# Transposed scores eight groups behind the maxima instead of ten, in an attention and feed-forward kernel on one core

## What is computed

```
h = x @ W1 + b1;  q, k, v = h by heads (16 heads, 8 wide)
w = softmax(where causal: q . k / sqrt(8));  y = x + (w . v) @ Wp + bp
h = (y - mean(y)) / sqrt(var(y) + eps)
prev = h shifted by one token
xr = mu_r * h + (1 - mu_r) * prev;  xk = mu_k * h + (1 - mu_k) * prev
z = h + sigmoid(xr @ Wr.T) * (relu(xk @ Wk.T) ** 2 @ Wv.T)
out = (z - mean(z)) / sqrt(var(z) + eps)
```

## Time and profile before

| | |
|---|---|
| runs, median (lowest to highest) | 651.06 us (650.29 to 652.81) |
| profiled execution | 650.12 us |
| its span, first to last instruction | 648.4 us |
| granted TensorE clock, mean | 0.976 |
| busy: TensorE, VectorE, ScalarE, GpSimd | 564.7, 550.0, 451.1, 413.6 us |
| weight loads of TensorE | 243.9 us |
| chain that ended last, by engine | TensorE 38%, VectorE 28%, GpSimd 14%, ScalarE 7%, issue 6%, DMA 5% |

### The profile page before, as it was taken

How to read it: one execution, slowest core, us unless ns; L and a number is a source line. 1 busy time by engine, 2 the same in 40 slices (tenths; PEclk the granted TensorE clock), 3 DMA queues, 4 the chain that set the end, 5 groups by cost and what they waited for, 6 DMA issues and landing times.

```text
span 648.4 us, 17196 instructions
## 1 busy us (share of the span) xinstructions
PE 564.7 (87%) x6438; PEld 243.9 (38%) x6438; DVE 550.0 (85%) x1579; ACT 451.1 (70%) x878; POOL 413.6 (64%) x576
## 2 busy tenths in 40 slices
PE   3457888999999999999999999999999999997864
PEld 1122333444343534343443444343434344342333
DVE  1477789999999999999999999999999999894437
ACT  2102777777787878787878778787878787776831
POOL 4100425667778686767767786867777777757673
PEclk9999999999999999999999999999999999997965
DMA  4652262525355443726264545436362535410101
GB/s 169 116 148 51 84 135 77 140 52 149 85 148 101 134 101 116 134 85 135 51 168 81 149 103 147 95 125 116 117 126 64 133 66 148 85 37 3 33 17 33
DMA packets 70825, 65.78 MB, mean 101 GB/s; under 512 B 14357, under 2 KB 60502, under 8 KB 70742
## 3 DMA queue, kind: packets, MB, share of 16 engines
q1 hardware_dynamic: 70178, 64.22, 41.2%
q10 hardware_dynamic: 564, 0.46, 0.3%
HBM read 34.70 MB, written 29.88 MB: 100 GB/s over the span
## 4 chain that ended last, share of the span: by engine, by line
PE 38%; DVE 28%; POOL 14%; ACT 7%; issue 6%; DMA 5%; SPq 2%; DVEq 0%; POOLq 0%; ACTq 0%
DVE rowmax L813 16%; PE ops L606 12%; PE sps L579 8%; POOL probs L1021 6%; PE tps L541 5%; PE spare L502 4%; POOL scaled L1059 4%; PE sps L564 4%; ACT probs L730 3%; POOL mixed L1063 3%; PE spare L482 3%; PE spare L516 2%; DMA d_parts<-qk_parts 2%; DVE stats L819 2%; DVE attnT L876 2%
## 5 line engine op out<-in xcount | busy, mean ns | idle before, releaser
L813 DVE TENSOR_REDUCE rowmax<-sps 128x1 f32<-128x512 f32 (+7 forms) x1024 | 395.6, 444 | 36.0 <-PE sps L579 34.7
L730 ACT ACTIVATE probs<-tps 128x512 f32<-128x512 f32 x640 | 347.6, 598 | 98.0 <-PE tps L541 95.4
L1021 POOL TENSOR_SCALAR_AFFINE_SELECT probs<-probs 128x512 f32<-128x512 f32 x256 | 158.6, 637 | 172.8 <-ACT probs L730 172.2
L606 PE MATMUL ops<-probs,vop 128*32 128x384 f32 (+3 forms) x2048 | 173.7, 446 | 15.9 <-ACT osum L736 8.1
L579 PE MATMUL sps<-kop,qop 48*64 48x512 bf16 (+7 forms) x2048 | 130.0, 309 | 12.1 <-DMA kop<-d_parts 12.1
L541 PE MATMUL tps<-qop,kop 50*128 50x384 bf16 (+3 forms) x1024 | 126.7, 306 | 12.3 <-ACT probs L730 11.6
L564 PE MATMUL sps<-qmask,dup 64*128 64x128 bf16 (+1 forms) x640 | 69.8, 215 | 28.2 <-DVE rowmax L813 25.9
L541 PEld LDWEIGHTS tps<-qop,kop 50*128 50x128 bf16 x1024 | 34.2, 94 | 147.7 <-ACT probs L730 122.8
L606 PEld LDWEIGHTS ops<-probs,vop 128*32 128x32 f32 x2048 | 50.4, 109 | 79.5 <-issue 41.5
L579 PEld LDWEIGHTS sps<-kop,qop 48*64 48x64 bf16 x2048 | 43.0, 106 | 53.4 <-issue 21.7
L564 PEld LDWEIGHTS sps<-qmask,dup 64*128 64x128 bf16 x640 | 31.3, 94 | 75.2 <-DVE rowmax L813 70.7
(11 more groups left out here) (111 smaller groups left out, 501.0 us busy)
## 6 DMA issues: line engine op xcount, KB each, us to landing
qop<-d_parts SPq DMA_DIRECT2D x64, 192.0 KB, 4.5
kop<-d_parts SPq DMA_DIRECT2D x63, 192.0 KB, 5.0
d_parts<-qk_parts SPq DMA_DIRECT2D x15, 768.0 KB, 3.4
d_parts<-qk_parts SPq DMA_DIRECT2D x15, 512.0 KB, 4.6
d_parts<-qk_parts SPq DMA_DIRECT2D x17, 256.0 KB, 4.6
xT<-x_by_channel SPq DMA_DIRECT2D x16, 256.0 KB, 2.6
xres<-x SPq DMA_DIRECT2D x16, 256.0 KB, 3.5
out<-result SPq DMA_DIRECT2D x15, 256.0 KB, 2.5
```

The costliest lines, as they stand in the source:

```text
L606: last = nc.tensor.matmul(ops[32 * t:32 * t + 32, BLK * a:SEQ], vop[:, par, a, QUARTET * half + t, hh, :], probs[:, g % 2, i, off:off + w] ...
L730: nc.scalar.activation(probs[:, g % 2, i, :], tps[:, bank(n), :], ACT.Exp, scale=SCALE)\
L813: last = nc.vector.reduce_max(rowmax[:, par, QUARTET * half + i, a:a + 1], sps[:, bank(n), off:off + w], axis=AX_X)
L1021: last = nc.gpsimd.affine_select(out=v, in_=v, compare_op=ALU.is_ge, fill=0.0, base=0, pattern=[[0, QUARTET], [1, BLK]], channel_multiplie ...
```

## The change

It sets `LEAD` to 2, so the stages T, D, E and F run two groups earlier against S. A is split: making q and k stays with A, now one step sooner (offset 3, groups 8 and 9, first step -3), while storing, splitting and loading their parts is a stage L with the old offset. Against the transposed scores, q and k, their splits, project, key, gate and hT keep their groups; v0 goes from late group 6 to 5, v1 from 9 to 6, value from 5 to 9. On VectorE and GpSimd, transposing and splitting the maxima go ahead of their group's work; z, its moments and its inverse deviation come four, two and one groups later (z behind value); both halves of `h` are made in late group 6. On GpSimd the second scaling of the mixing goes from late group 9 to 0 and its sum to 1, the bias sum to 3, the square to 5. On ScalarE `copy_o` goes ahead of the group's spare use. On SP the load of the residual input goes behind the maxima of half 0, and the loads of half 0's operands no longer wait until half of the maxima are made. The core of the diff:

```diff
-OFFSET = {"X": 3, "A": 2, "S": 1, "T": 0, "D": -1, "E": -2, "F": -3}
-FIRST_STEP, LAST_STEP = -2, 17
+OFFSET = {"X": 3, "A": 3, "L": 2, "S": 1, "T": 0, "D": -1, "E": -2, "F": -3}
+FIRST_STEP, LAST_STEP = -3, 17
...
-    ("A", "q"): (0, 0), ("A", "k"): (1, 0),
-    ("S", "v0"): (6, 0), ("S", "v1"): (9, 0),
+    ("A", "q"): (8, 0), ("A", "k"): (9, 0),
+    ("S", "v0"): (3, 0), ("S", "v1"): (4, 0),
     ("D", "project"): (4, 0), ("D", "hT"): (7, 0),
-    ("E", "key"): (2, 0), ("E", "gate"): (3, 0), ("E", "value"): (5, 0),
+    ("E", "key"): (2, 0), ("E", "gate"): (3, 0), ("E", "value"): (9, 0),
...
-LEAD = 0
+LEAD = 2
...
# SP
-                    if active("S", b):
-                        wait(sp, s_done, 4 * GROUPS * before("S", b) + 2 * GROUPS)
...
                 if active("S", b):
                     load_max(other, 0, 2 * before("S", b))
+                if active("D", b + 1):
+                    wait(sp, xbias_done, before("D", b + 1))
+                    sp.dma_start(xres[:], ...).then_inc(xres_in, 16)
...
# ScalarE
-                        for _, use, n in ORDER[b, g, place]:
-                            spare_use(use, n)
                         if place == 0 and tg == 1 and active("D", tb):
                             copy_o(before("D", tb), 1)
                         if place == 0 and tg == CHUNKS + 1 and active("T", tb):
                             copy_o(before("T", tb), 0)
+                        for _, use, n in ORDER[b, g, place]:
+                            spare_use(use, n)
...
-                    if g in (2, 3) and active("A", b) and before("A", b) > 0:
-                        split_middle(before("A", b), g - 2)
+                    if g in (0, 1) and active("L", b):
+                        split_middle(before("L", b), g)
...
# VectorE
+                    if g == CHUNKS and active("S", b):
+                        turn_maxima(before("S", b), 0)
+                    if g == 0 and active("S", b - 1):
+                        turn_maxima(before("S", b - 1), 1)
                     if active("S", b):
                         reduce_chunk(before("S", b), g, 0)
                         reduce_chunk(before("S", b), g, 1)
-                    if g == CHUNKS and active("S", b):
-                        turn_maxima(before("S", b), 0)
-                    if g == 0 and active("S", b - 1):
-                        turn_maxima(before("S", b - 1), 1)
...
-                    if tg == 4 and active("D", tb) and before("D", tb) < LAST:
+                    if tg == 5 and active("D", tb) and before("D", tb) < LAST:
...
                         layer_norm_moments(y, 0, n, stats_done, moments_done)
-                    if tg == 9 and active("E", tb) and before("E", tb) < LAST - 1:
-                        n = before("E", tb)
+                    if tg == 6 and active("D", tb) and before("D", tb) < LAST:
+                        n = before("D", tb)
+                        wait(dve, z_done, n - 1)
+                        for half in range(2):
+                            normalise(0, n, half, y, h[:, n % 2], rstd_done, h_done)
+                    if tg == 1 and active("F", tb) and before("F", tb) < LAST - 1:
+                        n = before("F", tb)
                         wait(dve, z_done, n + 1)
                         layer_norm_moments(z, 1, n, stats2_done, moments2_done)
```

More of the change, by code:

```diff
@@ L408, in step @@
                 par, other = b % 2, 1 - b % 2
-                if active("D", b):
-                    wait(sp, xbias_done, before("D", b))
-                    sp.dma_start(xres[:], x[b + OFFSET["D"]].rearrange("(t p) e -> p t e", p=P)).then_inc(xres_in, 16)
                 if active("S", b):
@@ L421, in step @@
                     load_max(par, 1, 2 * before("T", b) + 1)
-                if active("X", b):
+                if active("X", b) and before("X", b) > 0:
                     n = before("X", b)
@@ L425, in step @@
                     sp.dma_start(xT[:, n % BANKS], xT_in[b + OFFSET["X"]]).then_inc(xT_loaded[n % BANKS], 16)
-                if active("A", b) and before("A", b) == 0:
+                if active("L", b) and before("L", b) == 0:
                     for i in range(2):
@@ L437, in step @@
                     load_operand(sp, par, 0, 1, 0)
-                elif active("A", b):
-                    n = before("A", b)
+                elif active("L", b):
+                    n = before("L", b)
                     wait(sp, qk_split, 2 * (n + 1))
@@ L456, in step @@
                     load_max(other, 0, 2 * before("S", b))
+                if active("D", b + 1):
+                    wait(sp, xbias_done, before("D", b + 1))
+                    sp.dma_start(xres[:], x[b + 1 + OFFSET["D"]].rearrange("(t p) e -> p t e", p=P)).then_inc(xres_in, 16)
                 if active("F", b) and before("F", b) < LAST:
@@ L612, in step @@
             def step(b):
-                if b == 1 - OFFSET["A"]:
+                if b == -OFFSET["L"]:
                     setup_rest()
@@ L751, in step @@
             def step(b):
[L752 to L755, removed]
                 for g in range(GROUPS):
                     tb, tg = late(b, g)
+                    if (b, g) == (-OFFSET["L"], 2):
+                        act.wait_ge(first_out[1], 48)
+                        load_operand(act, 0, 0, 1, 1)
+                        setup_rest()
                     for place in range(2):
@@ L888, in step @@
                     tb, tg = late(b, g)
-                    if active("S", b):
-                        reduce_chunk(before("S", b), g, 0)
-                        reduce_chunk(before("S", b), g, 1)
                     if g == CHUNKS and active("S", b):
@@ L895, in step @@
                         turn_maxima(before("S", b - 1), 1)
+                    if active("S", b):
+                        reduce_chunk(before("S", b), g, 0)
+                        reduce_chunk(before("S", b), g, 1)
                     for _, use, n in ORDER[b, g, 0]:
@@ L906, in step @@
                         divide(before("T", tb), 0)
-                    if tg == 6 and active("D", tb) and before("D", tb) < LAST:
-                        normalise(0, before("D", tb), 1, y, h[:, before("D", tb) % 2], rstd_done, h_done)
                     if active("S", b):
@@ L1067, in step @@
                     tb, tg = late(b, g)
+                    if g == CHUNKS and active("S", b):
+                        split_max(before("S", b), 0)
+                    if g == 0 and active("S", b - 1):
+                        split_max(before("S", b - 1), 1)
+                    if g == 2 and active("L", b):
+                        split_low(before("L", b), 1)
+                    if tg == 0 and active("F", tb) and before("F", tb) < LAST - 1:
+                        n = before("F", tb)
+                        is_read(pool, "value", n)
+                        wait(pool, result_done, n)
+                        nc.gpsimd.tensor_tensor(z[:].rearrange("p t e -> p (t e)"), gated[:],
+                                                h[:, n % 2].rearrange("p t e -> p (t e)"), ALU.add).then_inc(z_done, 1)
                     if tg == 0 and active("E", tb) and before("E", tb) < LAST:
+                        mix_scale(before("E", tb), 0)
+                    if tg == 1 and active("E", tb) and before("E", tb) < LAST:
                         mix_add(before("E", tb), 0)
[L1070 to L1075, removed]
+                    if tg == 3 and active("D", tb):
                         n = before("D", tb)
@@ L1083, in step @@
                                                 ALU.add).then_inc(xbias_done, 1)
-                    if tg == 3 and active("E", tb) and before("E", tb) < LAST:
+                    if tg == 5 and active("E", tb) and before("E", tb) < LAST:
                         n = before("E", tb)
@@ L1087, in step @@
                         nc.gpsimd.tensor_tensor(ksq[:], krelu[:], krelu[:], ALU.mult).then_inc(ksq_done, 1)
-                    if tg == 5 and active("D", tb) and before("D", tb) < LAST:
+                    if tg == 6 and active("D", tb) and before("D", tb) < LAST:
                         inverse_deviation(0, before("D", tb), moments_done, vareps_done, rstd_done)
[L1090 to L1095, removed]
                     if tg == 8 and active("D", tb) and before("D", tb) < LAST:
@@ L1100, in step @@
                         mix_add(before("D", tb), 1)
-                        mix_scale(before("D", tb), 0)
                     if active("T", tb):
                         mask_group(before("T", tb), tg)
-                    if g == 3 and active("A", b):
-                        split_low(before("A", b), 0)
-                    if g == CHUNKS and active("S", b):
-                        split_max(before("S", b), 0)
-                    if g == 0 and active("S", b - 1):
-                        split_max(before("S", b - 1), 1)
+                    if tg == 2 and active("F", tb) and before("F", tb) < LAST - 1:
```

(4 more changed lines are left out.)

6 lines of the change are left out of this document (removed).

## The result

The changed kernel takes 662.29 us (661.02 to 664.9, four runs) where the kernel before, on the same chip, takes 650.67 (the three runs and a fourth, 649.69): a ratio of 1.0179, 95% interval 1.0139 to 1.022. It is slower by 11.6 us; 3.9 us faster was forecast. The profiled execution took 662.04 us with a span of 660.3, so the spans differ by 11.9.

The account below looks back on a forecast made before the run. The prediction took TensorE and VectorE to bound the kernel in turns, neither full. Its terms, -8.4-0.5-0.7+8.6-0.8-1.0-1.1 = -3.9, took 651.06 to 647.2, said as 647 us, range 638 to 654.

Parts of the forecast that it names:

- VectorE has 25.2 us of work: Steady batch, rest of k to the maximum freeing late group 9: 25.2 us against 25.5 before, so no difference there.
- GpSimd's other moves lie in its idle time: GpSimd, busy 26.0 of 35.3 us: its moves cost nothing; without that cover late masks hold output matmuls up to 1.3.
- The fill: Before the first transposed score: q and k hidden, v0's 0.24 gained, transposed scores sooner; -8.4, bounds -5.5 to -9.
- Late group 9: Last group of a batch's transposed scores: first mask to next batch 3.32, before 2.60; +0.72 a batch, +8.6 over 12.
- The waits: TensorE's waits for mask (0.19) and output copy (0.53) vanish but gain nothing; about 0.5 for a maximum in late groups 2, 3.
- Batch 0: First batch of transposed scores: late group 1 meets a short pair, -0.5.
- Batches 1 and 14: Batch 1 has no value, gated or z yet, -0.7; batch 14 has no q and k, -0.8 (-2.5 to +0.7).
- Batch 15: Last batch: its first two groups now run beside maxima groups 8 and 9; -1.0 (-3 to +1).
- rival 1: Steady batches: VectorE alone sets the step, a batch stays at 35.3; 638.6 us, chance 0.22.
- The rule weighed: Judging TensorE by weight loads makes VectorE the limit and the 0.72 vanish: -12.5 in place of -3.9; not followed.
- Rival 2: Late group 0: half 0's maxima come back late, TensorE waits about 1 us in 14 batches; 660 us, chance 0.12.
- Rival 3: Fill: q and k not hidden, start not sooner, the fill gives 5.5; 650 us, chance 0.13.

Follow-up runs that it names:

- both edits: Changed kernel with GpSimd's bias sum back in late group 2 and its late group 6 mask waiting for both halves of h: 643.33 us, ratio 0.9874.
- experiment three: The run of both edits, made to the changed kernel: 643.33 us, ratio 0.9874 to the kernel before.
- experiment nine: From experiment six, value moved from late group 9 to late group 8: 653.14 us, ratio 1.0018.
- experiment two: Changed kernel with only GpSimd's mask of late group 6 made to wait for both halves of h: 653.94 us, ratio 1.0043.
- experiment six: From experiment three, the moments of z put ahead of the rest of k on VectorE in late group 1: 634.83 us, ratio 0.976.
- experiment seven: From experiment three, value moved to late group 5, v0 and v1 to late groups 8 and 9: 675.18 us, ratio 1.0387.
- a third: The edit of experiment six on top of both edits, run again with more rounds: 634.92 us, ratio 0.9737.

## Why the prediction was wrong

**The step that failed** is "VectorE has 25.2 us of work", with "GpSimd's other moves lie in its idle time" at nothing. The 25.2 was summed from durations that the division and `h` have while GpSimd leaves them alone. Whether they keep them depends on what GpSimd does at that moment, and the change moved both engines' work. They measured 0.79 and 0.64 a batch more, 1.43 in all: from the rest of k to that maximum VectorE is busy 26.8 us in the changed kernel (348.31 to 375.87) and 25.4 with both edits (341.88 to 368.01 of experiment three), and idle 0.7 in both, where 1.1 was counted. For GpSimd's moves I asked who waits for their results (late masks, up to 1.3) and not whom they hold up while they run.

The Trainium skill (SBUF — State Buffer, Who interferes with whom) states this: VectorE and GpSimd share a pair of ports, a VectorE instruction with two SBUF inputs contends with a GpSimd one that reads SBUF and not with one that only writes, a tensor_scalar from and to SBUF can contend too (in its faster two-port modes), a tensor_reduce never, and the second to issue waits for the first. The traces agree for the division beside the bias sum (1.20), beside the square (0.82) and beside the write (0.42), and for `h` beside the mask (0.66); the reductions, which here read PSUM and not SBUF, keep their durations within 0.06 beside any of them. They differ in one point, and there the measurement decides: GpSimd's scaling also reads SBUF and doesn't block the division, as these rows of the kernel before show (GpSimd, then VectorE); in all fourteen batches where it lies within a scaling it takes 0.41.

```profile
405.95 1.57 POOL L1059 TENSOR_SCALAR scaled<-step_d,scalars 128x512 f32<-128x512 f32 x1
```
```profile
407.00 0.41 DVE L869 TENSOR_TENSOR attn<-turned,inv 128x256 f32<-128x256 f32 x1
```

**The fill was right**: -8.4 forecast, -8.93 measured. The first score matmul of the maxima starts at 21.70 (21.82 before), so the rest of k costs nothing and the bound of -9 is nearly reached.

**Late group 9 was right in itself.** From its first mask matmul to the next batch it takes 379.24-375.92 = 3.32, as summed from the earlier trace rows:

```profile
375.92 0.23 PE L562 MATMUL sps<-qmask,dup 64*128 64x128 bf16 x2 [0.17 <-DVE rowmax L809]
376.08 0.41 PE L577 MATMUL sps<-kop,qop 48*64 48x384 bf16 x8
376.42 1.16 PE L480 MATMUL spare<-value_weights,ksq 128*128 128x128 f32 x8
...
379.24 0.39 PE L539 MATMUL tps<-qop,kop 50*128 50x512 bf16 x2
```

Taking value out there wins only 0.40 of its 1.09, though, as experiment nine shows; in late group 8 all of it counts. Without the collisions the batch is 35.82 where 36.0 was forecast, +0.50 in place of +0.72, since late group 9's mask then starts 32.5 us after the batch's start, 0.2 sooner than before, where no difference was forecast. Experiment three's 643.33 is 8.2 under its kernel before, where 3.9 was forecast: the steps of the working stood but for the missing term, the sizes only roughly.

**The waits** went as foretold: those of the earlier trace rows nearly vanish, the waits for the maxima grow instead, and late groups 2 and 3 wait 0.27 and 0.28 for a maximum (about 0.5 forecast).

**The other terms.** Batch 0: -0.5 forecast, -1.0 measured. Batches 1 and 14: -0.7 and -0.8 forecast, +0.75 and +0.29 measured; late group 7 in each is as long as in the middle (3.94 and 3.99), so `h`'s 0.64 is in both. At the end of batch 1 the granted clock falls besides (0.83 in 116.00 to 119.04), and late group 9 takes 3.96 where experiment two, with the clock at 1.00, has 3.50. Without either, in experiment two, batches 1 and 14 take 34.52 and 33.95, 0.36 under the kernel before: half of what was forecast. Batch 15: -1.0 forecast, -0.22; its cause was not followed. The end: -1.1 forecast, -1.23.

**The rivals.** VectorE alone as the limit (rival 1) falls, and so does TensorE alone: experiment six won 0.77 from VectorE's order with TensorE's work as it was; experiment seven lost 0.64 in late group 8 by v0, which is no work of VectorE, and experiment nine 1.09 there by value, where VectorE then idles 0.46 for TensorE (`gated` moved along with value). They take turns, group by group. The rule weighed, of the Trainium skill (Perfetto Trace Analysis, Identifying the Most-Contended Engine), would have made the 0.72 vanish; the 3.32 above and the +0.50 a batch without the collisions show that most of it did not. In that section the Trainium skill goes by the share of TensorE's peak rate (MFU) as well as by weight loads; the prediction took the latter alone. Rival 2, the late maxima, has the sign and nearly the size (660), but not the cause: TensorE waits for their load once, 1.16 us ahead of batch 1, and in no steady batch. Its working also misread: the 0.44 is the time in which SP's queue issues a load, and such a load lands 5.0 us (median) after its issue. In the changed kernel the load back of the maxima is issued at 375.03, 4.21 ahead of the transposed score that it is for, at 379.24. Rival 3 falls with the fill.

## What to carry to other kernels

Before you move work on VectorE or GpSimd, list what the other one runs in that microsecond, and look in the trace for the same instruction beside it: one operation with two durations (0.41 and 0.81 here, a mean of 452 ns in place of 414) is the sign. A rise in an engine's busy time with the same instructions was, here, a wait in disguise. And when an order loses, look for the collision before you undo the order: this one, with two edits, is 1.3% faster than the kernel before, and with a third 2.6%.

## What the runs showed of the hardware

- A blocked division ends 0.28 us after the GpSimd operation that it met, for the bias sum as for the square, where alone it takes 0.41. The mask and `h` take turns: the first mask is stretched too, 0.71 in place of 0.63, and each blocked `h` ends 0.08 after a mask.
- Why GpSimd's scaling blocks nothing while its sums and masks do was not tried and stays open.
- With value in late group 8, nothing but scores and output stands at the end of a batch, and at six seams of two batches the granted clock then fell to 1.2 GHz for about 3 us, 1.0 to 1.3 us a batch. With value in late group 9 (experiment six) it fell in none of batches 2 to 13. That the emptier stretch is the cause is not shown: the undisturbed seams are as empty (2.08 of 3.00 us busy). What decides it, in seven of twelve batches and not in the others, stays open.
